# Writing out the attention loop over pairs of batches, on all five engines

## The reference

```python
x = x + attention(layernorm(x), Wq, bq, Wk, bk, Wv, bv, Wo, bo, relative_k, relative_v)   # 16 heads of 8
x = x + ffn(layernorm(x), router_w, router_b, w1, b1, w2, b2, sw1, sb1, sw2, sb2)

# attention, with rel_pos = r - l + 127 as an index into tables of 255 rows
scores = einsum('bhld,bhrd->bhlr', Q, K) / sqrt(8) + einsum('bhld,lrd->bhlr', Q, relative_k[rel_pos])
attn = softmax(scores)
out = (einsum('bhlr,bhrd->bhld', attn, V) + einsum('bhlr,lrd->bhld', attn, relative_v[rel_pos])) @ Wo.T + bo

# ffn: two shared experts, and eight of which each row takes its best two
ffn = (sum of 2 shared experts) / 2 + sum over the row's 2 best experts of softmax(gates) * expert
expert(h) = gelu(h @ w1 + b1) @ w2 + b2     # 128 -> 256 -> 128
```

## Time and profile before

| | |
|---|---|
| median of 3 runs | 2423.11 us (2423.08 to 2423.45) |
| the profiled execution | 2420.84 us |
| its span | 2419.0 us |
| TensorE products busy | 2281.8 us (94%) |
| TensorE weight loads busy | 1539.8 us (64%) |
| VectorE busy | 1813.4 us (75%) |
| ScalarE busy | 1528.8 us (63%) |
| GpSimd busy | 1066.7 us (44%) |
| instructions in the trace | 91053 |

### The profile page before, as it was taken

One profiled execution on the slowest core, in us unless ns is written; L12 is line 12 of the kernel. 1 busy time (PEld: TensorE's weight loads), 2 busy tenths in 40 slices (PEclk: granted clock), 3 DMA queues, 4 the chain that ended last, 5 costly groups with the idle time before them and its releaser, 6 DMA issues.

```text
span 2419.0 us, 91053 instructions
## 1 busy us (share of the span) xinstructions
PE 2281.8 (94%) x37474; PEld 1539.8 (64%) x37474; DVE 1813.4 (75%) x3479; ACT 1528.8 (63%) x3354; POOL 1066.7 (44%) x975
## 2 busy tenths in 40 slices
PE   4999999999989999999999999999989898988988
PEld 2666666666666666666666666666666666666666
DVE  5777776777767777867777777777767887888876
ACT  4666666666656666665666566666646666766666
POOL 3433443343334433433443344334416565656656
PEclk8999999999999999999999999999999999999999
DMA  4113112211221131122112211221112111111210
GB/s 124 39 42 82 48 49 54 70 49 45 63 62 45 49 76 48 49 59 67 49 40 61 73 49 40 76 54 43 49 43 29 18 22 17 22 25 14 26 18 10
DMA packets 249561, 114.75 MB, mean 47 GB/s; under 512 B 140170, under 2 KB 245012, under 8 KB 249204
## 3 DMA queue, kind: packets, MB, share of 16 engines
q1 hardware_dynamic: 249204, 109.59, 18.6%
HBM read 83.34 MB, written 8.39 MB: 38 GB/s over the span
## 4 chain that ended last, share of the span: by engine, by line
PE 81%; DVE 13%; issue 3%; SPq 1%; ACT 1%; POOL 0%; DMA 0%; DVEq 0%; POOLq 0%; ACTq 0%
PE ps L1194 20%; PE ps L1155 11%; PE ps L1211 8%; PE ps L1221 8%; PE ps L1162 8%; PE ps L1173 7%; DVE q_f L913 3%; DVE pick L950 2%; PE ps L1360 2%; PE ps L1361 2%; PE ps L1362 2%; PE ps L1377 2%; PE ps L1379 2%; PE ps L1378 2%; PE ps L1230 2%
## 5 line engine op out<-in xcount | busy, mean ns | idle before, releaser
L774 DVE TENSOR_REDUCE neg_max<-ps 128x2 f32<-128x1024 f32 x512 | 623.9, 1219 | 161.9 <-PE ps L1162 161.4
L559 ACT ACTIVATE probs<-ps,neg_max 128x512 f32<-128x512 f32 x1024 | 689.8, 680 | 71.9 <-DVE neg_max L774 71.6
L423 POOL TENSOR_TENSOR stat_hi<-q_twice,mask8h 128x1024 f16<-128x1024 f16 x128 | 243.2, 1900 | 1006.6 <-PE ps L1162 981.1
L549 ACT ACTIVATE probs_t<-ps 128x512 f32<-128x512 f32 x512 | 305.1, 596 | 498.8 <-PE ps L1194 498.6
L1194 PE MATMUL ps<-const,probs 128*128 128x128 f32 x4096 | 572.2, 280 | 16.9 <-DVE q_rel L759 8.5
L780 DVE COPY probs_t<-ps 128x512 f32<-128x512 f32 x512 | 352.3, 688 | 273.0 <-PE ps L1194 272.3
L1194 PEld LDWEIGHTS ps<-const,probs 128*128 128x128 f32 x4096 | 448.5, 142 | 134.9 <-issue 99.9
L482 POOL TENSOR_TENSOR probs_t<-probs,probs_t 128x1024 f16<-128x1024 f32 x160 | 341.3, 2133 | 194.2 <-ACT probs_t L639 193.9
L1155 PE MATMUL ps<-keys,stat_hi 128*32 128x512 f16 x4096 | 316.5, 386 | 0.0
L1162 PE MATMUL ps<-rk_split,stat_rel 96*32 96x512 f16 (+1 forms) x4096 | 284.3, 353 | 0.0
L633 ACT ACTIVATE probs<-ps,b_s 128x512 f32<-128x512 f32 x320 | 210.9, 688 | 104.2 <-PE ps L1362 102.2
(11 more groups left out here) (130 smaller groups left out, 2928.7 us busy)
## 6 DMA issues: line engine op xcount, KB each, us to landing
rv_step<-in_rv_win SPq DMA_DIRECT2D x128, 512.0 KB, 3.8
keys<-keys SPq DMA_DIRECT2D x64, 96.0 KB, 2.2
x_pair<-in_x SPq DMA_DIRECT2D x8, 512.0 KB, 4.2
q_twice<-q_hi SPq DMA_DIRECT2D x32, 128.0 KB, 2.4
q_lo_pair<-q_lo SPq DMA_DIRECT2D x32, 128.0 KB, 2.4
rel_scratch<-rel_t SPq DMA_DIRECT2D x128, 32.0 KB, 2.8
x_pair<-in_x SPq DMA_DIRECT2D x16, 256.0 KB, 3.2
x_pair<-rel_scratch SPq DMA_DIRECT2D x64, 64.0 KB, 4.0
```

Source lines behind the costliest of these rows:

```text
L549: nc.scalar.activation(probs_t[s % 2][:, 2 * p, :, :].rearrange("p r c -> p (r c)"), ps[:, TR_BANK, :], ACT.Copy).then_inc(evac_act, 1)
L559: nc.scalar.activation(probs[:, q, :], ps[:, bank + q % 2, :], ACT.Exp, bias=neg_max[:, q:q + 1], accum_out=row_sum[parity][:, s * QUADS + ...
L774: nc.vector.tensor_reduce(neg_max[:, 2 * p:2 * p + 2], ps[:, bank:bank + 2, :], op=ALU.max, axis=AX_X, negate=True).then_inc(max_done, 1)
```

## The change

On each of the five engines the loop of the engine becomes a loop of Python, so its body is issued three times with the pair's number as a constant. Nothing else is edited: the functions that are called, their arguments' meaning, the order on each queue, the semaphores' counts and the FFN loops stay.

```diff
             pair_windows(0, 0, True, True)
-            with sp.Fori(0, PAIRS // 2 - 1) as i:
+            for i in range(PAIRS // 2 - 1):
                 pair_windows(2 * i + 1, 1, False, True)
                 pair_windows(2 * i + 2, 0, False, True)
             pair_windows(PAIRS - 1, 1, False, False)
...
-            with pool.Fori(0, PAIRS // 2 - 1) as i:
+            for i in range(PAIRS // 2 - 1):
                 pair_steps(2 * i + 1, False, True)
                 pair_steps(2 * i + 2, False, True)
...
-            with act.Fori(0, PAIRS // 2 - 1) as i:
+            for i in range(PAIRS // 2 - 1):
                 pair_steps(2 * i + 1, 1, False, True)
                 pair_steps(2 * i + 2, 0, False, True)
...
-            with dve.Fori(0, PAIRS // 2 - 1) as i:
+            for i in range(PAIRS // 2 - 1):
                 pair_steps(2 * i + 1, 1, False, True)
                 pair_steps(2 * i + 2, 0, False, True)
...
-            with pe.Fori(0, PAIRS // 2 - 1) as i:
+            for i in range(PAIRS // 2 - 1):
                 pair_steps(2 * i + 1, 1, False, True)
                 pair_steps(2 * i + 2, 0, False, True)
```

## The result

| | median | runs | profiled execution, span |
|---|---|---|---|
| before | 2422.54 us | 2421.52 to 2423.45, 6 runs | 2420.84, 2419.0 us |
| changed | 2436.02 us | 2434.82 to 2438.70, 6 runs | 2436.72, 2434.9 us |

The ratio is 1.0058, 95% interval 1.0045 to 1.0071. The forecast was 2411, between 2406 and 2416. The kernel got slower by 13.5 us where a gain of 12 was forecast.

A forecast was written before the change was run, and what follows sets the result against it. TensorE's queue and its standstills were taken as the bound (busy 94%, 81% of the chain). From 2423.11 us, -11.75 for the back edges and -0.54 for register work, together -12.3, gave 2410.8, so 2411; range 2406 to 2416.

The forecast's parts named there:

- The two back edges: Attention loop's two taken branches on TensorE: idle time and lower clock behind them vanish in straight code, 11.75 us saved.
- the register work: Attention loop's register instructions vanish with constant pairs; sum -0.54 us, between -1.3 and +0.7.
- The clean pairs: Pairs 1 and 6, untouched by a taken branch, at 218.72 and 218.63 us; the measure for pairs 2 to 5.
- The three terms of the register work: ScalarE over six pairs: step 1, slot 0 -0.78; step 13, slot 1 -0.48; step 11, slots 0 and 2 +0.72 us.
- The tail of lower clock: Behind each back edge, in pairs 3 and 5, TensorE's clock is lower; 1.63 and 2.33 us, all saved.
- the stall: TensorE's idle time before a back edge's next scores, in pairs 2 and 4; 4.04 and 3.75 us, saved.
- the half-gain rival: The stall goes but the lower clock falls elsewhere in the attention part; 2415 us, chance 7%.
- VectorE, ScalarE and GpSimd at the borders: At the pair borders their own branches and fetches are covered by TensorE's; if not, the saving is smaller by 8 us.
- Everything after pair 7 is the same code: FFN loop and what follows are unedited; over six turns the clock's effect evens out: 0, with 2 us either side.
- The rival that said so: Slower: moved FFN loop lies over one block too many on some engine, fetched at six back edges; 2439 us, 4%.
- The price of that rival: FFN loop's refetch priced as the far branch, 4.7 to 5.0 less 0.2 us; 6 x 4.6 = 28 us.
- The rule on branches: Cited for the FFN loop: an engine keeps two 16 KiB blocks (128 KiB on TensorE); branching out costs a fetch.

The follow-up runs named there:

- with 4 memsets: Changed kernel plus four one-column memsets on VectorE's queue in pair 7; 2412.27 us.
- the turn longer by 96: Changed kernel with four memsets on VectorE in pair 7 and 96 one-column memsets inside VectorE's FFN turn, experts 3 to 9; 2412.84 us.
- with 112: Changed kernel plus 112 one-column memsets on VectorE's queue in pair 7; 2410.84 us.
- all but VectorE: Kernel before with the attention loop written out on TensorE, ScalarE, GpSimd and SyncE, kept as a loop on VectorE; 2411.94 us.
- the kernel before with 24 more: Kernel before, all loops kept, plus 24 memsets on VectorE's queue in pair 7; 2437.04 us.

## Why the prediction was wrong

*The two back edges, -11.75, and the register work, -0.54.* Right, nearly to the tenth. Pairs 1 to 6 took 1323.8 us before and take 6 x 218.60 = 1311.6 now, -12.2 against -12.3. The clean pairs were the right measure. The clean pairs give the split: pair 1 went from 218.72 to 218.60 and pair 6 from 218.63 to 218.60, and three times 0.12 and three times 0.03 are 0.45 us of register work, which leaves 11.75 for the edges. The three terms of the register work came out too: ScalarE idles 0.38 us at step 1, slot 0 in all six pairs, 1.97 at step 13, slot 1 (read in pair 2), and step 11, slots 0 and 2 take 4.42 us each. Where the FFN loop stayed loaded, the kernel with the attention written out was 9 to 12 us faster than before: 9.1 with 4 memsets, 9.4 with the turn longer by 96, 12.3 with 112. The tail of lower clock went with the stall, as forecast: the half-gain rival didn't come about.

*VectorE, ScalarE and GpSimd at the borders.* VectorE's fetch is mostly covered, as forecast: it is worth 1.0 us, by the run with all but VectorE. For ScalarE and GpSimd no run shows it apart.

*Everything after pair 7 is the same code, "I take 0".* This is the step that failed. The code is the same, its place is not, and the place decides whether a loop stays loaded. It measured +23.0 in the six turns. The rival that said so was there, with its mechanism and its sign (a packet on an instruction queue inside the FFN loop), at 2439; measured was 2436. Its chance of 4% was the error. The argument against it read VectorE's turn as 181 instructions. The sequencer's are missing there; the trace has 270, and 181 could never touch a fourth block of 128, while 270 can. The rest of the argument, that the turn had fitted "without a single packet, so there is no sign of a tight fit", takes one throw for a margin. A turn of 270 instructions on blocks of 128 needs a fourth block at 13 of 128 places, one in ten, and before it had been some 15 places from that. This could be counted beforehand. The trace of before has the packets' size, the instructions of a turn, and pair 7 as the pattern for how many instructions a written-out pair has; what it lacked was the offset of the first block and how many blocks stay, and so one in ten would have been a fair estimate of the chance.

*The price of that rival, 4.6 us a turn, 28 in all.* Too high by a fifth. It was TensorE's far branch; VectorE's costs 2.5 to 2.7 us more than a near one in the changed kernel, and some 2.2 to 2.5 more where the next border comes two instructions later, of which some is hidden: 23.0 / 6 = 3.8 us in the changed kernel, 14.1 / 6 = 2.4 in the kernel before with 24 more, where the border is farther on. That the rival's sum comes so close is luck: it has 28 - 12.3 = 15.7 us over before, the profiles have 15.9, but of these only 23.0 are the turns; 2.8 are the start (see below), and 2.3 pair 7 and what follows the loop, for which it had no term.

*The range.* The ends that the prediction lists add up to 2408 and 2418, not to 2407 and 2415: at the least 7.8 of the edges, +0.7 and +2 give 2423.1 - 5.1 = 2418. It made no difference here.

*No term for the start.* Start and pair 0 are 2.8 us longer in the changed kernel's profile, with the same instructions. It isn't the change: with 112 memsets more pair 0 starts at 44.26 and takes 213.26 us, as before. The granted clock is 0.50 from 44 to 52 us in the changed kernel and 1.00 from 48 us on in that one (first the changed kernel, then the one with 112 more):

```profile
44.00:48.00 4.00, 3.32 (x41) 1.05 (x45) 0.87 (x1) 0.00 (x0) 4.00 (x7) 0.50 0.01 4
48.00:52.00 4.00, 3.15 (x41) 1.07 (x33) 1.58 (x2) 2.89 (x8) 1.72 (x1) 0.50 0.00 0
```

```profile
44.00:48.00 4.00, 3.76 (x49) 1.08 (x49) 1.41 (x2) 0.41 (x1) 4.00 (x6) 0.61 0.02 4
48.00:52.00 4.00, 2.90 (x45) 1.68 (x49) 2.46 (x3) 3.25 (x10) 0.93 (x1) 1.00 0.00 0
```

TensorE had been idle nearly 14 us before either, and pair 0 comes out between 213.2 and 216.0 us in the profiles of the twelve kernels. What moves the clock's return from one execution to the next isn't settled here.

*The rule on branches.* "Runtime: NRT & Kernel Launch" of the Trainium skill, section Instruction fetch mechanics, says that a taken branch out of the loaded window forces a fetch of the target before execution goes on. The traces agree, for TensorE (4.7 to 5.0 us) and for VectorE (2.91 us behind the branch, in the chain above). Its sizes don't hold for VectorE here. With two blocks of 256 instructions, a head at 126 or 254 can be slow only at one of the two, and 128 instructions more would have cured the changed kernel; they didn't, and the packets are 8 KB. Room for three blocks of 128 fits all eleven kernels that keep the FFN loop. Why five packets come in a turn that touches four blocks stays open.

## What to carry to other kernels

Writing a loop out moves all code behind it. Count, for every loop that stays, the instructions of a turn on each engine (the sequencer's too) against that engine's blocks, and look for packets on the instruction queues inside the loop: none means it stays loaded, some at each back edge means that a few instructions of padding ahead of it, here four, can be worth more than the edit. And when a long loop is written out, expect the gain of the engine whose turn doesn't stay loaded, here TensorE's 5 to 6 us a back edge with the lower clock behind it, and write out what follows as well or check its place.

## What the runs showed of the hardware

- VectorE's code is fetched in packets of 8 KB, and its place repeats with 128 instructions (480.5 and 482.8 us for six turns, 457.3 with 4 more). A turn that touches three such blocks stays loaded (ends at 380: 457.4 us, no packet), one that touches four is fetched again each time (ends at 392: 472.2 us, five packets a turn).
- From the start of VectorE's branch to its target it is 2.8 to 3.3 us in the FFN loops that are fetched again, 3.4 to 4.1 us at the attention's back edges (3.46 and 4.00 before), and 0.27 to 0.36 us where the turn stays loaded. The next block is another 2.2 to 2.5 us behind the first where it is wanted at once (2.45 in the chain above).
- TensorE's FFN turn, some 1440 instructions, stays loaded in all eleven kernels that keep the loop: q8 has no packet between 1890 and 2330 us.
- 96 memsets of one column in VectorE's FFN turn cost nothing: 457.3 us for six turns with them and without.
